# Perceiver block: reordering the first batch of an interval (statistics of x1, a state sum, norm rows and transposes)

## The chip, the cores and the metric

The kernel runs on one core of one Trainium2 chip. The metric is the device time of one execution in microseconds (us), as the median of several runs. Five engines with a queue each matter here: TensorE (PE, its weight loads are shown as PEld), VectorE (DVE), ScalarE (ACT), GpSimd (POOL) and SyncE (SP), which here only starts transfers. Each engine works through its own queue in order and waits on semaphores for the others.

## What is computed

```python
x = x + cross_attention(ctx, ctx, layernorm(x), mask)   # 64 batches, 32 rows, 257 keys, 16 heads of 32
x = x + mamba(layernorm(x))                             # below
x = x + quantised_ffn(layernorm(x))                     # 512 -> 2048 -> 512

# mamba: d_inner 1024, 16 states, over the 32 rows of each batch
x_, z = split(x @ in_proj_w)                            # 512 -> 2 * 1024
x_ = silu(causal_conv4(x_) + conv_b)
Bm, C, d = split(x_ @ x_proj_w)                         # 16, 16, 1
dt = softplus(d * dt_w + dt_b)
h[s] = exp(dt * A) * h[s-1] + (dt * x_) * Bm            # 16 states for each channel
y = sum_n(h * C) + x_ * D
out = (y * silu(z)) @ out_proj_w
```

## The kernel before

The 64 batches are 16 tiles of 4 batches (128 rows). Attention works batch by batch, mamba tile by tile. The two are interleaved by hand: `interval(ta, tm, to, more)` is one stretch in which the four batches `b = 0..3` of tile `ta` pass through attention, while tile `tm = ta - 1` begins mamba ("front") and tile `to = ta - 2` finishes it ("back"). The 16 intervals are followed by a hand-written tail and by the feed-forward part. Intervals 2 to 15 have both a front and a back. These are the 14 that the diff touches in full.

`schedule` is one function that every engine runs with its own class of parts (`Loads` for SP, `Products` for PE, `Functions` for ACT, `Side` for POOL, `Elementwise` for DVE). A part that an engine doesn't define does nothing there. So the order of the calls in `interval` is the order of the work in each of the five queues, and moving one call moves it in every queue that has a part of that name.

The scan of a tile goes by 8 chunks `c` of 128 channels. Each chunk has four steps on DVE, written (c, op): op 0 multiplies u with B (L1779), op 1 is the scan over 128x2048 elements (L1784), op 2 the product with C (L1790), op 3 the sum over the 16 states (L1756 twice and L1761). After op 2 POOL starts a transfer that adds one half of the states onto the other (L1527), so op 3 has 8 states left for all chunks but the last. `CHAIN` is the order of the 32 steps. `DONE` is a step's place in it, which the semaphore `scan_step` counts. Two chunk buffers alternate. `FINISH` and `BEGIN` say at which named place of which batch a step stands: `place("s")`, `place("a")` and so on. `FINISH_DECAYS` and `BEGIN_DECAYS` do the same for the exponentials of ACT (L1433) that feed op 1.

The parts that the diff moves, all in the first batch (`b == 0`):

- `mamba_norm(tm)`: DVE takes the statistics of x1 (BATCH_NORM_STATS L1577, BATCH_NORM_AGGREGATE L1582). POOL makes the inverse standard deviation and the shift out of them (`rstd`: L1488, L1490, L1493).
- `mamba_rows(tm)`: ACT writes the normed rows into `ln_out` (L1291).
- `mamba_turn`: PE transposes them into bank 5 (L1085). `mamba_transpose`: ACT copies them to `xn2T` (L1348). `mamba_in` (PE, L1092) multiplies them with the input weights; it waits for `xn2T` and for `keys_copy`.
- `keys_copy(g+1, 0)`: ACT copies half of the next batch's keys out of bank 6 (L1265).

Around them stand `x1_write` (DVE, L1693: attention's output plus residual), `load_bias` and `residual` (SP loads four bias rows, L789; POOL adds them to x, L1516, giving `xbo` for the next tile), `scores` (PE L1021, DVE score passes L1666), `softmax` (ACT exponentials L1286, then the DVE reciprocal L1679), `normalise` (ACT L1323), `kv_keys` (PE L988; POOL scales the mask, L1502), `kv_values` (PE L999), `transpose_p` (PE L1030) and `mamba_keep` (POOL copies x1 to x2, L1555).

Of the kernel before, what the change touches and what calls it, by code (L numbers as in the profile page):

```python
# [39 lines left out]
def perceiver_kernel(nc, x, ctx_kv, mask, Wq, bq, Wk, bk, Wv, bv, Wo, bo, Win, conv_w, conv_b, Wx,  # L40
# [13 lines left out]
    with ExitStack() as ctx:  # L54
# [270 lines left out]

        CHAIN = [(0, 0), (0, 1), (0, 2)]
        for c in range(1, IC):
            CHAIN += [(c, 0), (c, 1), (c, 2), (c - 1, 3)]
        CHAIN.append((IC - 1, 3))
        DONE = {step: k + 1 for k, step in enumerate(CHAIN)}  # L330
        FINISH = {(0, "a"): range(21, 22), (0, "b"): range(22, 26), (0, "c"): range(26, 28),
                  (1, "a"): range(28, 29), (1, "t"): range(29, 31), (1, "p"): range(31, 32)}
        BEGIN = {(1, "w"): range(0, 1), (1, "d"): range(1, 3), (1, "e"): range(3, 4), (2, "a"): range(4, 5),
                 (2, "b"): range(5, 7), (2, "c"): range(7, 9), (2, "d"): range(9, 11), (2, "e"): range(11, 12),
# [100 lines left out]
        def schedule(part, engine):  # L435
# [22 lines left out]
            def interval(ta, tm, to, more):  # L458

                here, front, back = ta is not None, tm is not None, to is not None  # L460
                for b in range(BT):
                    following = here and (b < BT - 1 or more)
                    g = ta * BT + b if here else None
                    keys = DC * (g + 2) if following else 0

                    def place(name):
                        if back:
                            part.decays(to, FINISH_DECAYS.get((b, name), ()))
                            part.scans(to, FINISH.get((b, name), ()))
                        if front:  # L470
                            part.decays(tm, BEGIN_DECAYS.get((b, name), ()))
                            part.scans(tm, BEGIN.get((b, name), ()))
                        if not front and not back:
                            part.weights_prepare(b, name)

                    if b == 0 and front:
                        part.x1_write(tm)
                    if b == 0 and here:
                        part.load_bias(ta)
                        part.residual(ta)  # L480
                    if following and 0 < b < BT - 1:
                        part.kv_turn(g + 1, 0, 0)
                    if here:
                        part.scores(g, ta, b, to)
                    if b == 0 and front:
                        part.mamba_norm(tm)
                    if b == 1 and front:
                        part.mamba_bcd(tm, keys - DC)
                    if following and 0 < b < BT - 1:
# [36 lines left out]
                        part.q_spread(ta + 1)  # L526
                    if following:
                        part.kv_keys(g + 1, b, ta, tm, to, more)
                    if following:
                        part.keys_copy(g + 1, 0)  # L530
                    if following and b == 0:
                        part.kv_values(g + 1, 0, range(0, 2))
                    if here:
                        part.normalise(g)
                    if b > 0:
                        place("n")
                    if b == 0 and front:
                        part.mamba_rows(tm)
                    if following:
                        part.keys_copy(g + 1, 1)  # L540
                    if b == 0 and front:
                        part.mamba_turn(tm, keys)
                        part.mamba_transpose(tm, keys)
                    if b == 0:
                        place("n")
                    place("k")
# [71 lines left out]
                    if b == 3 and here:  # L618
                        part.wo_product(ta, keys)

            interval(0, None, None, True)
            interval(1, 0, None, True)
            interval(2, 1, 0, True)
            with engine.Fori(3, NT - 1) as t:
                interval(t, t - 1, t - 2, True)
# [1377 lines left out]
```

## Time and profile before

| | |
|---|---|
| median of 3 runs | 2046.67 us (2040.75 to 2046.87) |
| the profiled execution | 2044.58 us, of which the span is 2042.8 us |
| mean granted TensorE clock | 0.977 |
| one interval in the steady part | about 110.2 us |

The profiled execution is 2.1 us below the median of the three and inside their range. Busy shares of the span: PE 93%, DVE 91%, ACT 82%, POOL 24%. A busy share doesn't say which engine sets the pace: for that the waits of each engine in one interval are read, and the timeline around the place that is changed. Below, "T" is the start of `x1_write` (L1693) in an interval.

### The profile page before, as it was taken

To read this page: it belongs to the slowest core of one execution; us is meant where nothing else is said; L and a number is where in the kernel's file an instruction comes from. 1 tells how busy PE (TensorE), PEld (TensorE's weight loads), DVE (VectorE), ACT (ScalarE), POOL (GpSimd) and SP (SyncE) were. 2 spreads that over 40 slices of the span, in tenths; PEclk is the share of its full clock that TensorE was granted. 3 is DMA by queue.
4 is the path that set the end of the run, shared out by engine and by line. 5 is a ranking of instruction groups with operands and counts; after the bars stand their busy time and mean duration, and the time that the engine had idled before them with its cause. 6 is when DMAs were issued, how large, how long until landed. Compare 5 with 4: busy or idle time off the path is not lost.

```text
span 2042.8 us, 37585 instructions
## 1 busy us (share of the span) xinstructions
PE 1907.6 (93%) x11658; PEld 1352.9 (66%) x11658; DVE 1850.1 (91%) x2315; ACT 1681.6 (82%) x4617; POOL 496.9 (24%) x397
## 2 busy tenths in 40 slices
PE   8898999999999999999999999999999999568799
PEld 5576776767676666767676767676667767366444
DVE  1546999999999999999999999999999999999778
ACT  3458989898988989898989898988989898876483
POOL 1001213041423223141314142423314141201013
PEclk9999999999999999999999999999999999788899
DMA  9523333333332333333333334233333233320214
GB/s 285 219 83 89 78 91 78 84 84 103 72 106 67 84 91 83 93 83 90 77 91 81 97 72 114 66 86 93 72 93 85 91 86 83 98 73 11 73 43 142
DMA packets 93395, 188.53 MB, mean 92 GB/s; under 512 B 18768, under 2 KB 39904, under 8 KB 88160
## 3 DMA queue, kind: packets, MB, share of 16 engines
q1 hardware_dynamic: 78448, 133.32, 20.2%
q0 software_dynamic: 14832, 54.01, 14.1%
q8 instruction: 32, 0.52, 0.1%
q14 instruction: 83, 0.68, 0.1%
HBM read 116.12 MB, written 17.18 MB: 65 GB/s over the span
## 4 chain that ended last, share of the span: by engine, by line
PE 43%; ACT 16%; DVE 12%; issue 11%; POOL 3%; SPq 1%; DMA 1%; DVEq 0%; POOLq 0%; ACTq 0%
PE bank L1092 10%; PE bank L999 8%; ACT dA L1433 7%; PE bank L1133 5%; PE bank L988 5%; DVE hb L1784 5%; PE bank L1196 3%; PE bank L1218 3%; PE bank L1039 2%; DVE hb L1779 2%; DVE hb L1756 2%; ACT xD L1417 2%; PE bank L1119 1%; POOL stats L1490 1%; DMA bo_sb<-bias_dram 1%
## 5 line engine op out<-in xcount | busy, mean ns | idle before, releaser
L1433 ACT ACTIVATE dA<-dt,A_sb 128x124 f32<-128x124 f32 x2048 | 617.1, 392 | 9.6 <-DVE dt L1734 8.4
L1784 DVE TENSOR_TENSOR_SCAN hb<-dA,hb 128x2048 f32<-128x2048 f32 x118 | 522.5, 4428 | 8.5 <-ACT dA L1433 4.8
L988 PE MATMUL bank<-ctxT,wk_sb 128*128 128x256 f32 x2048 | 463.1, 384 | 14.8 <-ACT ctxT L1249 11.4
L999 PE MATMUL bank<-wv_sb,ctxT 128*128 128x512 f32 x1024 | 465.4, 595 | 2.3 <-ACT ctxT L1249 2.3
L988 PEld LDWEIGHTS bank<-ctxT,wk_sb 128*128 128x128 f32 x2048 | 383.9, 191 | 78.9 <-ACT ctxT L1249 18.2
L999 PEld LDWEIGHTS bank<-wv_sb,ctxT 128*128 128x128 f32 x1024 | 186.7, 191 | 188.7 <-issue 185.3
L1527 POOL DMA_DIRECT2D hb<-hb x103 | 93.3, 906 | 861.5 <-DVE hb L1790 846.3
L1779 DVE TENSOR_TENSOR hb<-u,BC 128x2048 f32<-128x2048 f32 x118 | 270.4, 2291 | 5.7 <-DVE u L1746 2.6
L1790 DVE TENSOR_TENSOR hb<-hb,BC 128x2048 f32<-128x2048 f32 x117 | 268.9, 2298 | 1.5
L1092 PE MATMUL bank<-xn2T,win_sb 128*128 128x128 f32 x2048 | 237.9, 278 | 0.7 <-ACT xn2T L1348 0.7
L1092 PEld LDWEIGHTS bank<-xn2T,win_sb 128*128 128x128 f32 x2048 | 235.4, 194 | 4.2 <-issue 2.2
L1502 POOL TENSOR_SCALAR maskn<-maskb 128x257 f32<-128x257 f32 x64 | 140.2, 2191 | 270.1 <-DVE soft L1666 267.7
L1756 DVE TENSOR_TENSOR hb<-hb 128x512 f32<-128x512 f32 (+2 forms) x248 | 149.7, 604 | 4.6
L1039 PEld LDWEIGHTS bank<-PT,V 128*128 128x128 f32 x1024 | 124.8, 194 | 35.2 <-issue 35.2
L1272 ACT COPY V<-bank 128x512 f32<-128x512 f32 x128 | 75.0, 586 | 77.0 <-PE bank L1039 55.7
L1286 ACT ACTIVATE Pr<-Pr,soft 128x257 f32<-128x257 f32 x256 | 127.3, 510 | 12.1 <-DVE soft L1666 11.9
L1249 ACT ACTIVATE ctxT<-bank,lastT 128x256 f32<-128x256 f32 x256 | 102.3, 474 | 36.5 <-PE bank L954 34.3
L1265 ACT ACTIVATE KT<-bank,bqkv 128x256 f32<-128x256 f32 x256 | 106.2, 467 | 29.7 <-PE bank L988 28.5
L1039 PE MATMUL bank<-PT,V 128*128 128x128 f32 x1024 | 127.5, 278 | 2.0 <-ACT PT L1340 2.0
L1323 ACT ACTIVATE Pr<-Pr,soft 128x256 f32<-128x256 f32 x256 | 109.2, 506 | 14.0 <-DVE soft L1679 14.0
L1720 DVE SCALAR_TENSOR_TENSOR xs<-xpad,convw,xs 128x128 f32<-128x128 f32 x384 | 103.7, 347 | 14.7 <-ACT xs L1367 14.2
L1666 DVE CUSTOM_DVE_ANT_0 Pr<-bank,maskn 128x257 f32<-128x257 f32 x256 | 93.2, 421 | 17.7 <-PE bank L1021 17.5
(159 smaller groups left out, 2581.5 us busy)
## 6 DMA issues: line engine op xcount, KB each, us to landing
hb<-hb POOLq DMA_DIRECT2D x103, 512.0 KB, 4.8
ctx_sb<-in_ctx_dram SPq DMA_DIRECT2D x64, 512.0 KB, 3.7
BC<-bcd_dram SPq DMA_DIRECT2D x32, 1024.0 KB, 7.2
maskb<-in_mask_Bx1x1xS_fk_dram SPq DMA_DIRECT2D x64, 128.5 KB, 3.4
wstage<-in_L_ffn_w_dram SPq DMA_DIRECT2D x4, 2048.0 KB, 11.2
x_sb<-in_x_dram SPq DMA_DIRECT2D x16, 256.0 KB, 3.4
win_sb<-in_L_attn_in_proj_w_dram SPq DMA_DIRECT2D x1, 4096.0 KB, 24.3
bo_sb<-bias_dram SPq DMA_DIRECT2D x64, 64.0 KB, 2.0
```

The lines of the kernel that those rows point to most:

```text
L988: last = pe.matmul(bank[6 + j][:, (m % 2) * KF:(m % 2 + 1) * KF], wk_sb[:, c, m * P:(m + 1) * P], ctxT[:, c, :], start=(c == 0), stop=(c = ...
L999: last = pe.matmul(bank[h][:], ctxT[:, c, h * P:(h + 1) * P], wv_sb[:, c, :], start=(c == 0), stop=(c == DC - 1))
L1039: last = pe.matmul(bank[4][:, m * P:(m + 1) * P], V[:, h, m * P:(m + 1) * P], PT[:, h, m, :], start=(h == 0), stop=(h == 1))
L1092: last = pe.matmul(bank[6 + q % 2][:, e * P:(e + 1) * P], win_sb[:, c, n:n + P], xn2T[:, c, :], start=(c == 0), stop=(c == DC - 1))
L1286: act.activation(Pr[:, m, :], Pr[:, m, :], ACT.Exp, scale=-1.0, bias=soft[:, 0, m:m + 1], accum_out=soft[:, 1, m:m + 1]).then_inc(exp_done, 1)
L1323: act.mul(Pr[:, m, 0:KF], Pr[:, m, 0:KF], soft[:, 2, m:m + 1]).then_inc(p_ready, 1)
L1433: last = act.activation(dA[:, c % 2, n * BT:(n + 1) * BT, 1:], dt[:, c, :].rearrange("p (b s) -> p b s", s=S)[:, :, 1:], ACT.Exp, scale=A_ ...
L1502: pool.tensor_scalar(maskn[:], maskb[:], -NEG, 1.0, ALU.mult, ALU.mult).then_inc(mask_scaled, 1)
L1756: dve.tensor_tensor(tile[:, 0:n, :], tile[:, 0:n, :], tile[:, n:2 * n, :], ALU.add).then_inc(sum_step, 1)
L1779: ins = dve.tensor_tensor(tile, u[:, c, :].unsqueeze(1).broadcast_to([P, NS, P]), BC[:, 0:NS, :], ALU.mult)
L1784: ins = dve.tensor_tensor_scan(flat, dA[:, c % 2].rearrange("p n s -> p (n s)"), flat, 0.0, ALU.mult, ALU.add)
L1790: ins = dve.tensor_tensor(tile, tile, BC[:, NS:2 * NS, :], ALU.mult)
```

## The change

In the first batch of an interval the statistics of x1 (`mamba_norm`) come right behind `x1_write`, ahead of `residual` and of the score passes. The sum of chunk 4 stands ahead of the product with C of chunk 5, at the place "s" between the score passes and the reciprocal. The normed rows (`mamba_rows`) come right behind the exponentials on ACT, ahead of `normalise`; their transposes on PE come ahead of the first half of `kv_values`, and the copy to `xn2T` ahead of `keys_copy(g+1, 1)`. For that `keys_copy(g+1, 0)` moves behind `normalise` in the first batch; in the other batches its order against the engines' other work is as before.

```diff
         for c in range(1, IC):
-            CHAIN += [(c, 0), (c, 1), (c, 2), (c - 1, 3)]
+            CHAIN += [(c, 0), (c, 1), (c - 1, 3), (c, 2)] if c == 5 else [(c, 0), (c, 1), (c, 2), (c - 1, 3)]
...
-        FINISH = {(0, "a"): range(21, 22), (0, "b"): range(22, 26), (0, "c"): range(26, 28),
+        FINISH = {(0, "s"): range(21, 22), (0, "a"): range(22, 23), (0, "b"): range(23, 26), (0, "c"): range(26, 28),
...
                     if b == 0 and front:
                         part.x1_write(tm)
+                        part.mamba_norm(tm)
...
                     if here:
                         part.scores(g, ta, b, to)
-                    if b == 0 and front:
-                        part.mamba_norm(tm)
...
                     if following:
                         part.kv_keys(g + 1, b, ta, tm, to, more)
-                    if following:
-                        part.keys_copy(g + 1, 0)
+                    if b == 0 and front:
+                        part.mamba_rows(tm)
+                        part.mamba_turn(tm, keys)
                     if following and b == 0:
                         part.kv_values(g + 1, 0, range(0, 2))
+                    if b > 0 and following:
+                        part.keys_copy(g + 1, 0)
                     if here:
                         part.normalise(g)
+                    if b == 0 and following:
+                        part.keys_copy(g + 1, 0)
                     if b > 0:
                         place("n")
                     if b == 0 and front:
-                        part.mamba_rows(tm)
+                        part.mamba_transpose(tm, keys)
                     if following:
                         part.keys_copy(g + 1, 1)
-                    if b == 0 and front:
-                        part.mamba_turn(tm, keys)
-                        part.mamba_transpose(tm, keys)
```

## Rows read from the trace of the kernel before

**Rows 1.** Busy time by interval: stretch, length, then each engine; one steady interval.

```profile
562.00:672.00 110.00, 106.48 (x663) 76.30 (x662) 107.15 (x134) 98.44 (x281) 31.08 (x24) 1.00 0.34 86
```

**Rows 2.** Waits of DVE, 562 to 672 us: total, times, longest.

```profile
DVE soft L1679 <- ACT Pr L1286: 0.7, 1, 0.7
...
DVE u L1746 <- DVE zs L1863: 0.2, 1, 0.2
```

**Rows 3.** Chain that ended last, 560 to 675 us: start, length, what.

```profile
574.69 0.66 POOL xbo L1516
```

**Rows 4.** Timeline of DVE from 572 us: start, length, engine, line.

```profile
572.31 0.67 DVE L1693 TENSOR_TENSOR x<-bank,xbo 128x512 f32<-128x512 f32 x1
...
572.89 0.42 DVE L1666 CUSTOM_DVE_ANT_0 Pr<-bank,maskn 128x257 f32<-128x257 f32 x1
...
574.27 0.69 DVE L1577 BATCH_NORM_STATS2 stats<-x 128x6 f32<-128x512 f32 x1
...
575.11 0.18 DVE L1582 BATCH_NORM_AGGREGATE stats<-stats 128x2 f32<-128x6 f32 x1
...
575.97 0.18 DVE L1679 RECIPROCAL soft<-soft 128x4 f32<-128x4 f32 x1 [0.68 <-ACT Pr L1286]
576.09 2.29 DVE L1790 TENSOR_TENSOR hb<-hb,BC 128x2048 f32<-128x2048 f32 x1
...
578.30 1.15 DVE L1756 TENSOR_TENSOR hb<-hb 128x512 f32<-128x512 f32 x2
...
579.80 2.29 DVE L1779 TENSOR_TENSOR hb<-u,BC 128x2048 f32<-128x2048 f32 x1
```

**Rows 5.** The same timeline: ACT and PE around the transposes.

```profile
573.86 0.51 ACT L1286 ACTIVATE Pr<-Pr,soft 128x257 f32<-128x257 f32 x1
...
576.54 1.71 ACT L1323 ACTIVATE Pr<-Pr,soft 128x256 f32<-128x256 f32 x4
...
577.64 1.88 PE L999 MATMUL bank<-wv_sb,ctxT 128*128 128x512 f32 x4
...
580.67 0.63 PE L1085 MATMUL bank<-idf,ln_out 128*128 128x128 f32 x4 [1.15 <-ACT ln_out L1291]
...
581.42 0.59 ACT L1348 COPY xn2T<-bank 128x512 f32<-128x512 f32 x1 [0.27 <-PE bank L1085]
...
582.15 7.38 PE L1092 MATMUL bank<-xn2T,win_sb 128*128 128x128 f32 x64
```

**Rows 6.** Timeline, 1289 to 1296 us: from a tile's statistics to POOL's power.

```profile
1291.42 0.18 DVE L1582 BATCH_NORM_AGGREGATE stats<-stats 128x2 f32<-128x6 f32 x1 [0.15 <-DVE stats L1577]
...
1291.79 2.46 POOL L1490 TENSOR_TENSOR stats<-stats,consts 128x1 f32<-128x1 f32 x1
```

**Rows 7.** Timeline, 653 to 673 us: score pass, its exponential, and rstd on POOL.

```profile
654.79 0.42 DVE L1666 CUSTOM_DVE_ANT_0 Pr<-bank,maskn 128x257 f32<-128x257 f32 x1
655.04 0.57 POOL L1490 TENSOR_TENSOR stats<-stats,consts 128x1 f32<-128x1 f32 x1
...
655.25 0.51 ACT L1286 ACTIVATE Pr<-Pr,soft 128x257 f32<-128x257 f32 x1 [0.39 <-DVE soft L1666]
...
655.82 0.26 POOL L1493 TENSOR_SCALAR stats<-stats 128x1 f32<-128x1 f32 x1 [0.21 <-POOL stats L1490]
```

**Rows 8.** Timelines where POOL and DVE meet: 241, 353, 564 and 2006 us.

```profile
241.29 1.27 POOL L1516 TENSOR_TENSOR xbo<-x_sb,bo_sb 128x512 f32<-128x512 f32 x1 [7.70 <-DVE x L1693]
...
353.21 2.96 DVE L1790 TENSOR_TENSOR hb<-hb,BC 128x2048 f32<-128x2048 f32 x1
...
564.52 0.93 POOL L1555 COPY x<-x 128x512 f32<-128x512 f32 x1
...
2006.42 1.05 DVE L1952 TENSOR_TENSOR w1qT<-w1qT 128x512 f32<-128x512 f32 x1
```

**Rows 9.** Durations of two DVE lines: count, ns min/median/max, first and last start.

```profile
L1761 DVE TENSOR_TENSOR u<-hb x117: 291/293/1128, 197.7 to 1786.3; 128x128 f32<-128x128 f32 x117
...
L1952 DVE TENSOR_TENSOR w1qT<-w1qT x16: 691/693/1477, 1989.4 to 2039.6; 128x512 f32<-128x512 f32 x16
```

## The prediction

> **What bounds the kernel now.** I read the busy time by interval first, then the waits inside one interval, then the chain, and last the timeline around T (the start of `x1_write`). In a steady interval PE is busy 106.5 of 110 us and DVE 107.2 [rows 1]. The two are too close for the shares to decide, so the waits must. DVE waits 0.7 us for ACT's exponentials before the reciprocal, and otherwise only for itself (0.2 us, the next largest) [rows 2]. PE waits 1.15 us for `ln_out` at the transposes alone [rows 5]. So DVE has about 0.7 us in each interval that another engine could give back, and PE has more. The chain runs through the place of the change: POOL makes `xbo` once the bias rows have landed, and only then come rstd, the normed rows and the transposes [rows 3]. That chain is one of several that are nearly tied. Since DVE hardly ever idles, its own queue is what an edit must shorten. I take DVE as the pace of intervals 2 to 15.
>
> **DVE before.** From T (572.31) to the multiply of chunk 6 (579.80) are 7.49 us [rows 4]: `x1_write`, four score passes, statistics, 0.68 us of waiting, reciprocal, product (5,2), sum (4,3).
>
> **DVE after, if nothing interferes.** `x1_write` takes 0.67; the statistics must now wait for it, and such a handover between dependent instructions costs some 0.04 (my estimate; bounds 0 and the 0.15 between the two statistics instructions [rows 6]). Then 0.69 + 0.15 + 0.18, so the statistics end at T+1.73. Four score passes take 1.38 (572.89 to 574.27), to T+3.11. The sum takes 1.50 from its start to the next start (578.30 to 579.80), some 0.1 less when the next instruction doesn't need it: T+4.5. Reciprocal 0.12, product 2.21 (576.09 to 578.30) [rows 4]: the multiply of chunk 6 starts at T+6.84, which is 0.65 earlier. The score passes were queued far ahead before and now stand behind a wait; I bound this by 0 and 0.15. The gain is 0.5 to 0.65.
>
> **Does the sum cover the wait?** A score pass starts 0.46 before its exponential when ACT is free [rows 7], so the exponentials start at T+2.2. From the first one to the reciprocal are 2.11 us (573.86 to 575.97) [rows 4, 5], so the reciprocal could go at T+4.3, with DVE busy until T+4.5. The wait of 0.68 is covered. The later score passes cost ACT only 0.6 us, since it was busy with decays until 573.86 anyway.
>
> **POOL.** rstd no longer stands behind `residual`. Statistics end to power takes 0.19 (1291.60 to 1291.79) [rows 6], the power 0.57, a gap 0.21, the last step 0.26 [rows 7]: rstd ends at T+2.96, where before PE stood waiting for the rows made from it until T+8.36 (580.67) [rows 5]. But `residual`, which ran from T+2.4 beside score passes and statistics, is now queued behind it. Its bias rows have landed by then (it ran from 574.69) [rows 3], so its 128x512 addition, 1.27 us long, runs from T+3.0 to T+4.25. Nobody waits for `xbo` soon. What matters is what DVE does then: the sum of chunk 4 starts at T+3.1.
>
> **What a large POOL operation costs DVE.** Beside score passes `xbo` costs nothing: 1.27 us at 241.29, and the passes keep their 0.42 [rows 4, 8]. Beside a DVE operation that reads two tensors from SBUF it costs much. The last add of a sum takes 0.29 us, but 1.13 where POOL's copy of 0.93 us starts within 0.03 us of it [rows 8, 9]; 14 of 117 are stretched so. It ends as if it had started 0.1 to 0.15 us before the end of the copy. And in one interval `xbo` itself came late, at 352.75: the product took 2.96 instead of 2.29 [rows 4, 8]. By the same reading the sum's first add now effectively starts at T+4.10 instead of T+3.1 to 3.25. It costs 0.85 to 1.0.
>
> The Trainium skill ("SBUF — State Buffer", Who interferes with whom) says that a DVE instruction with two SBUF inputs contends with a GpSimd instruction that reads SBUF, that whichever starts first keeps the port for the whole instruction, and that a DVE instruction with at most one SBUF input doesn't contend. The rows of `xbo` beside score passes, whose other input is in PSUM, agree. Where page and rows differ is the price: by the page DVE would wait for the whole 1.27 us, and the sum below would be 0.15 us an interval larger, +7.0 us in all.
>
> **Sum.** T+4.10 + 1.4 (sum) + 0.12 + 2.21 = T+7.83 against T+7.49: DVE loses 0.35 us an interval. Over 14 intervals this is +4.9 us. Their waits before the reciprocal are not all 0.7, and one of them already had the stretched product; I take these as cancelling within a microsecond. Interval 1 and the tail are taken at zero: interval 1 has no back, DVE idles there for many microseconds, and the tail isn't edited.
>
> **PE and ACT.** The normed rows follow the exponentials at about T+4.4 and end at T+5.2. `kv_keys` ends at T+5.33 (577.64), so the transposes follow it with hardly a wait, and the 1.15 us of idle PE time go [rows 5]. `normalise` waits for the reciprocal at T+5.6 and runs 1.7 us; then come `keys_copy` (two operations of the same width as `normalise`'s four, so 0.85) and the copy to `xn2T` (0.6) [rows 5]: `mamba_in` starts at about T+8.9 instead of T+9.84 (582.15). So PE is 0.9 us earlier, and what lies behind it (xpad, taps, convolution) is not late. Neither ACT nor PE becomes the bound; what they gain turns into waits for DVE, since DVE's queue sets the pace. `keys_copy(g+1, 0)` is some 2 us later, and it is next needed by `mamba_in` and by the scores of b = 1, 17 us on. I cost it at nothing.
>
> **Other queues.** SP's order is unchanged. POOL's transfer for chunk 5 is issued behind its product, some 0.4 us later, and the sum that needs it is 15 us away. The sum of chunk 4 comes 2.9 us earlier than before, but its transfer was issued at T-8. The scaled mask follows the transfer and still meets the multiply of chunk 6, as before.
>
> **Rivals.**
> 1. *The gain arrives.* POOL and DVE pass each other (`xbo` is held until the reciprocal or lands between instructions), and DVE keeps 0.5 to 0.65 us: -7 to -9 us. For it: the port is taken by whoever is first, and all depends on 0.1 us. Against it: I find no free 1.27 us on DVE before the product.
> 2. *The sum wins the port.* It starts before `xbo`, which is held and then takes a slice at the boundary between two adds. Such held operations stretch the next one by 0.36 (1.05 instead of 0.69) [rows 8, 9]. DVE then gains 0.15 to 0.3: -2 to -4 us.
> 3. *Slower.* The same mechanism at its worst. It gets dearer the closer behind the start of `xbo` the sum wants to start: if rstd ends 0.1 to 0.25 us later than I reckon while `xbo` is still first, the add is held until T+4.4. That is 0.3 more an interval, +0.65 x 14 = +9 us. It decides from a start of `xbo` at about T+3.1.
> 4. *PE was the pace* (through `ln_out`, as the chain suggests), and the whole 0.9 to 1.1 us come back: -13 to -15 us. Against it stands that DVE waits for others only 0.7 us in an interval.
> 5. *The change doesn't do what it says*: rstd early, but the normed rows don't come earlier, since ACT holds them back. They follow the exponentials directly, so I give this nothing of its own.
>
> **Numbers.** The profiled execution had 2044.58 us: 2044.6 + 4.9 = 2049.5. The median of three is 2.1 above it, which would give 2051.6. I say 2050. Chances: the forecast 0.42 (its own range 2047 to 2053), the gain 0.17, the sum first 0.17, slower 0.18, PE as the pace 0.06. The range is to leave out PE as the pace and the far ends of rivals 1 and 3: 2038 to 2056. A measurement of this kernel can tell about 0.3%, 6 us, from no change. Slower by more than that are rival 3 and a quarter of the forecast, 0.29; faster rival 4 and most of rival 1, 0.19; within it the rest, 0.52.
>
> **What the profile after would show.** DVE's wait before the reciprocal in batch 0 gone (right if below 0.1). The first add of the sum in batch 0 at 1.5 to 1.7 us instead of 0.69, beside `xbo` that starts at T+3.0. PE's wait for `ln_out` below 0.3. `mamba_in` at T+8.9. An interval of 110.5 us. It is wrong if the add keeps its 0.69 (rival 1: interval 109.6), if `xbo` itself is stretched beyond 1.27 (rival 2: 110.0), or if DVE idles elsewhere for ACT or PE, so that its queue wasn't the pace.

## The result and the profile after

| | before | after |
|---|---|---|
| median of 9 runs each | 2044.73 us (2040.75 to 2046.87) | 2049.48 us (2048.53 to 2053.39) |
| the profiled execution, its span | 2044.58 us, 2042.8 us | 2053.39 us, 2051.6 us |

The changed kernel takes 1.0028 times the time of the kernel before, with a 95% interval of 1.0018 to 1.0037: 4.75 us slower by the medians. The profiled execution of the changed kernel is the slowest of its nine, so the two profiles stand further apart (8.8 us in the spans) than the medians.

The busy time in one steady interval of the changed kernel (columns as in [rows 1]):

```profile
1238.12:1348.94 110.82, 106.81 (x664) 76.40 (x663) 108.30 (x134) 98.43 (x282) 27.99 (x24) 1.00 0.35 86
```

The interval is 110.8 us instead of 110.1 to 110.2. DVE's work has grown by 1.1 us (107.2 in [rows 1]), though its instructions are the same 134. The waits of one interval from T, DVE first and PE behind it (total, times, longest; they answer to [rows 2]):

```profile
DVE Pr L1667 <- issue: 0.4, 1, 0.4
DVE stats L1583 <- DVE stats L1578: 0.3, 2, 0.2
...
PE bank L989 <- ACT Q L1317: 0.8, 1, 0.8
PE bank L1120 <- ACT xs L1375: 0.4, 1, 0.4
PE bank L1093 <- ACT xn2T L1349: 0.4, 1, 0.4
```

DVE's wait for the exponentials is gone, as forecast. In its place stand 0.4 us before the first score pass, with "issue" as the cause: nothing that the profile shows held it. PE no longer waits a microsecond for `ln_out`, and has small new waits elsewhere, for ACT. The timeline of DVE from T = 1348.94 (it answers to [rows 4]; the columns are start, length, engine, line):

```profile
1348.94 0.67 DVE L1694 TENSOR_TENSOR x<-bank,xbo 128x512 f32<-128x512 f32 x1
1349.64 0.69 DVE L1578 BATCH_NORM_STATS2 stats<-x 128x6 f32<-128x512 f32 x1
1350.49 0.18 DVE L1583 BATCH_NORM_AGGREGATE stats<-stats 128x2 f32<-128x6 f32 x1 [0.15 <-DVE stats L1578]
...
1351.05 0.43 DVE L1667 CUSTOM_DVE_ANT_0 Pr<-bank,maskn 128x257 f32<-128x257 f32 x1 [0.38 <-issue]
...
1352.44 1.75 DVE L1757 TENSOR_TENSOR hb<-hb 128x512 f32<-128x512 f32 x1
...
1354.68 0.29 DVE L1762 TENSOR_TENSOR u<-hb 128x128 f32<-128x128 f32 x1
...
1354.89 0.17 DVE L1680 RECIPROCAL soft<-soft 128x4 f32<-128x4 f32 x1
...
1354.98 2.26 DVE L1791 TENSOR_TENSOR hb<-hb,BC 128x2048 f32<-128x2048 f32 x1
...
1357.16 2.28 DVE L1780 TENSOR_TENSOR hb<-u,BC 128x2048 f32<-128x2048 f32 x1
```

And POOL, ACT and PE in the same stretch:

```profile
1350.95 0.23 POOL L1489 TENSOR_SCALAR stats<-stats 128x1 f32<-128x1 f32 x1 [8.87 <-DVE stats L1583]
...
1351.27 0.57 POOL L1491 TENSOR_TENSOR stats<-stats,consts 128x1 f32<-128x1 f32 x1
...
1352.05 0.27 POOL L1494 TENSOR_SCALAR stats<-stats 128x1 f32<-128x1 f32 x1 [0.21 <-POOL stats L1491]
...
1352.37 1.27 POOL L1517 TENSOR_TENSOR xbo<-x_sb,bo_sb 128x512 f32<-128x512 f32 x1
...
1353.50 0.80 ACT L1292 ACTIVATE ln_out<-x,stats 128x512 f32<-128x512 f32 x1
1354.55 0.63 PE L1086 MATMUL bank<-idf,ln_out 128*128 128x128 f32 x4
...
1358.14 7.38 PE L1093 MATMUL bank<-xn2T,win_sb 128*128 128x128 f32 x64 [0.37 <-ACT xn2T L1349]
```

The reader is to see one pair: POOL's addition for `xbo` starts at T+3.43 and keeps its 1.27 us. The first add of the moved sum starts 0.07 us behind it and takes 1.75 us instead of 0.69 ([rows 9] have the same shape at 0.69). The multiply of chunk 6 starts at T+8.22, where it was at T+7.49 [rows 4] and in the second half of the trace before at T+7.48. The rows come at T+4.56, the transposes at T+5.61 instead of T+8.36, `mamba_in` at T+9.20 instead of T+9.84 [rows 5]. PE has what it was to get, and the kernel is slower.

### The profile page after: what moved, and what is told of

Read it like the earlier page. It is cut to its first block, busy times and chain, and to the rows that moved or that the text cites. A ratio compares the mean times of both kernels' runs of the same rounds, so it can differ in the third digit from the quotient of the medians.

```text
span 2051.6 us, 37558 instructions
## 1 busy us (share of the span) xinstructions
PE 1911.0 (93%) x11643; PEld 1353.3 (66%) x11658; DVE 1863.1 (91%) x2315; ACT 1679.7 (82%) x4617; POOL 451.8 (22%) x397
## 4 chain that ended last, share of the span: by engine, by line
PE 31%; DVE 29%; issue 23%; ACT 2%; DVEq 1%; DMA 0%; POOL 0%; POOLq 0%; ACTq 0%
DVE hb L1785 9%; DVE hb L1780 6%; PE bank L1093 5%; PE bank L989 5%; PE bank L1134 5%; PE bank L1000 5%; DVE hb L1757 5%; DVE xs L1721 3%; PE bank L1197 3%; PE bank L1219 3%; DVE u L1762 2%; DVE Pr L1667 1%; PE bank L1120 1%; PE bank L1040 1%; PE bank L1167 1%
## 5 line engine op out<-in xcount | busy, mean ns | idle before, releaser
L1434 ACT ACTIVATE dA<-dt,A_sb 128x124 f32<-128x124 f32 x2048 | 616.8, 391 | 12.7 <-DVE dt L1735 11.5
L1503 POOL TENSOR_SCALAR maskn<-maskb 128x257 f32<-128x257 f32 x64 | 125.3, 1958 | 269.5 <-DVE soft L1667 267.1
L1757 DVE TENSOR_TENSOR hb<-hb 128x512 f32<-128x512 f32 (+2 forms) x248 | 164.4, 663 | 4.9 <-DMA hb<-hb 0.3
L1721 DVE SCALAR_TENSOR_TENSOR xs<-xpad,convw,xs 128x128 f32<-128x128 f32 x384 | 103.1, 346 | 13.7 <-ACT xs L1368 13.4
L1489 POOL TENSOR_SCALAR stats<-stats 128x1 f32<-128x1 f32 x48 | 52.1, 1086 | 282.9 <-DVE stats L1583 282.9
## 6 DMA issues: line engine op xcount, KB each, us to landing
wstage<-in_L_ffn_w_dram SPq DMA_DIRECT2D x4, 2048.0 KB, 11.4
```

The costliest lines, as they stand in the source:

```text
L1434: last = act.activation(dA[:, c % 2, n * BT:(n + 1) * BT, 1:], dt[:, c, :].rearrange("p (b s) -> p b s", s=S)[:, :, 1:], ACT.Exp, scale=A_ ...
L1503: pool.tensor_scalar(maskn[:], maskb[:], -NEG, 1.0, ALU.mult, ALU.mult).then_inc(mask_scaled, 1)
L1721: dve.scalar_tensor_tensor(acc, src, tap, acc, ALU.mult, ALU.add).then_inc(conv_done, 1)
L1757: dve.tensor_tensor(tile[:, 0:n, :], tile[:, 0:n, :], tile[:, n:2 * n, :], ALU.add).then_inc(sum_step, 1)
```

## The experiments

All times are medians, each with its ratio to the kernel before on the same chip. T is the start of `x1_write` in an interval. The theory: DVE's queue is the pace, and the addition on POOL takes from it what the edit gave. The rivals: the new order of PE and ACT costs the time, the residual addition matters by its place in the chain before the rows, or PE is the pace.

**e4: the changed kernel with a one-column `xbo`.** The residual of the other columns is left out, from tile 1 on.

```diff
-                        pool.tensor_tensor(xbo[:], x_sb[:], bo_sb[:], ALU.add).then_inc(xbo_ready, 1)
+                        pool.tensor_tensor(xbo[:, 0:1], x_sb[:, 0:1], bo_sb[:, 0:1], ALU.add).then_inc(xbo_ready, 1)
```

> The changed kernel, but POOL adds bias and x for the first column only (the residual of the other 511 columns is left out, from tile 1 on). Order, waits and transfers are the same; only the length of the one POOL operation beside the sum goes, from 1.27 us to about 0.2. By the collision: 1.0 us less an interval, 13 to 15 us below the changed kernel, 8 to 11 below the kernel before in the profile. By the order of PE and ACT or by the statistics standing ahead: no more than 2 us below the changed kernel.

Measured: 2035.29 us, 0.9957 of before (0.9943 to 0.9971). That is 14 us below the changed kernel. POOL and DVE in its timeline:

```profile
1230.98 0.19 POOL L1517 TENSOR_TENSOR xbo<-x_sb,bo_sb 128x1 f32<-128x1 f32 x1
...
1231.05 1.15 DVE L1757 TENSOR_TENSOR hb<-hb 128x512 f32<-128x512 f32 x2
```

Both adds of the sum together take 1.15 us, where the changed kernel's take 2.21. The start is the same 0.07 us behind `xbo`. With the length of one POOL operation gone, everything else left as changed, the loss turns into a gain. The order of PE and ACT and the early statistics are still in this kernel, so neither can be what made the changed kernel slower than the kernel before.

**e1: the addition moved to where DVE leaves the port free.** The bias rows are loaded in the last batch of the interval before, and the addition goes ahead of rstd.

```diff
                     if b == 0 and front:
                         part.x1_write(tm)
-                        part.mamba_norm(tm)
                     if b == 0 and here:
-                        part.load_bias(ta)
+                        if isinstance(ta, int) and ta < 2:
+                            part.load_bias(ta)
                         part.residual(ta)
+                    if b == 0 and front:
+                        part.mamba_norm(tm)
...
+                    if b == 3 and here and more and not (isinstance(ta, int) and ta == 0):
+                        part.load_bias(ta + 1)
                     if b == 3 and back:
                         part.out_transpose(to, keys)
```

> The changed kernel, but with the residual addition back ahead of rstd on POOL, and with its four bias rows loaded at the end of the interval before (for the tiles from 2 on), so that the addition can start right behind x1_write, at T+0.8, and is over at T+2.1, before the sum of chunk 4 wants to start at T+3.5. PE's and ACT's order stay as changed. If the collision on the port of POOL and DVE makes the changed kernel slow: the first add of the sum is back from 1.76 to 0.69 us, DVE saves 1.07 us in each of 14 intervals, 13 to 15 us less than the changed kernel, some 5 to 10 below the kernel before. If the new order of PE and ACT (keys copied later, PE waiting for xn2T) is what costs: as slow as the changed kernel. If PE was the pace: 13 to 15 us below the kernel before.

Measured: 2036.06 us, 0.996 (0.9945 to 0.9974), 13.4 below the changed kernel and 8 below the kernel before. From T = 1335.38:

```profile
1336.38 1.27 POOL L1521 TENSOR_TENSOR xbo<-x_sb,bo_sb 128x512 f32<-128x512 f32 x1 [7.86 <-DVE x L1698]
...
1338.87 1.15 DVE L1761 TENSOR_TENSOR hb<-hb 128x512 f32<-128x512 f32 x2
...
1342.53 2.29 DVE L1784 TENSOR_TENSOR hb<-u,BC 128x2048 f32<-128x2048 f32 x1
```

The addition runs T+1.00 to T+2.27 beside the statistics and a score pass, and these keep their 0.69 and 0.42 us. The sum follows at T+3.49 unhindered. The interval is 109.75 us. All the work is done here, and the gain is e4's.

**e3: the sum back behind the product.** CHAIN and FINISH as before the change, all else as changed.

> The changed kernel with the sum of chunk 4 back behind the product (CHAIN and FINISH as before). Now the residual addition on POOL, T+3.4 to T+4.7, meets a DVE that waits for the exponentials. If DVE's queue is the pace: the add keeps its 0.69, but DVE waits 1.2 us before the reciprocal, the multiply of chunk 6 starts at T+8.5 instead of T+8.2, and the time is 3 to 6 us above the changed kernel. If PE is the pace: no slower than the changed kernel, since the transposes come as early as there.

Measured: 2055.25 us, 1.0051 (1.0037 to 1.0065), 5.8 above the changed kernel. Its DVE waits and its multiply of chunk 6 (T = 1239.55):

```profile
DVE soft L1680 <- ACT Pr L1287: 1.1, 1, 1.1
...
1248.07 2.29 DVE L1780 TENSOR_TENSOR hb<-u,BC 128x2048 f32<-128x2048 f32 x1
```

With nothing to do between the score passes and the reciprocal, DVE idles 1.1 us, and the multiply starts at T+8.52. PE's transposes come at T+5.6 as in the changed kernel, and it doesn't help. Moving the sum is worth 0.3 us an interval even with the collision. The early statistics without the sum, with the rest as changed, cost DVE 1.0 us: T+8.52 against T+7.48.

**e2: the sum alone.** CHAIN and FINISH as changed, all else as before.

> The kernel before with the sum of chunk 4 moved ahead of the product alone (CHAIN and FINISH). The score passes come at once behind x1_write, the statistics behind them, so the sum starts at T+3.0. The residual addition starts at T+2.0 to T+2.4 as before and overlaps the first 0.3 to 0.65 us of it. If DVE's queue is the pace: the wait of 0.68 for the exponentials goes, 0.15 to 0.5 of it is given back by the stretched add, so 0.2 to 0.5 less an interval, 3 to 7 us below the kernel before. If PE is the pace by way of the normed rows: no change, since PE and POOL wait as before.

Measured: 2099.68 us, 1.027 (1.0256 to 1.0285). This missed by 60 us, and neither theory had it. The first guess was the addition, which still overlaps the sum here. The next kernel takes it away.

**e5: the sum alone, with the bias rows early.** The diffs of e2 and, for the bias rows, of e1.

> The kernel before with the sum of chunk 4 ahead of the product, as in e2, and with the bias rows loaded an interval early, so that the residual addition on POOL is over at T+2.1, before the sum starts. The statistics stay behind the score passes, PE and ACT are as before. If the sum alone lost its time because the last one-column step of rstd on POOL, ready at about T+4.7, is held off the port by the product and the multiply that now follow each other without a gap: no help from the early bias rows; the step still ends at T+9 or later, and the time is 2085 to 2105 us. If it was lost to the residual addition beside the sum: some 2036 to 2040.

Measured: 2086.54 us, 1.0204 (1.0189 to 1.0219). With the addition out of the way 13 of e2's 55.5 us come back, where no help was expected; the other 42 stay. POOL and DVE in its timeline (T = 1258.56), and one interval's waits of DVE and PE:

```profile
1263.39 4.20 POOL L1496 TENSOR_SCALAR stats<-stats 128x1 f32<-128x1 f32 x1 [0.21 <-POOL stats L1493]
...
1263.08 2.26 DVE L1793 TENSOR_TENSOR hb<-hb,BC 128x2048 f32<-128x2048 f32 x1
1265.26 2.28 DVE L1782 TENSOR_TENSOR hb<-u,BC 128x2048 f32<-128x2048 f32 x1
...
DVE xs L1723 <- ACT xs L1370: 3.0, 2, 2.2
...
PE bank L1088 <- ACT ln_out L1294: 2.9, 1, 2.9
```

The last step of rstd works on one element in each partition and takes 0.26 us [rows 7]. Here it takes 4.20. It starts 0.31 us behind the product and ends with the multiply. In the second half of the kernel before it took 2.4 us:

```profile
1237.42 2.29 DVE L1790 TENSOR_TENSOR hb<-hb,BC 128x2048 f32<-128x2048 f32 x1
...
1238.00 2.36 POOL L1493 TENSOR_SCALAR stats<-stats 128x1 f32<-128x1 f32 x1 [0.21 <-POOL stats L1490]
...
1239.63 1.14 DVE L1756 TENSOR_TENSOR hb<-hb 128x512 f32<-128x512 f32 x2
```

The sum followed the product there, and the step ended at 1240.36, where one add waits for the other. In e2 and e5 the multiply follows, which depends on nothing just before it, and starts without a gap. In e5 the rows come at T+9.07, PE waits 2.9 us, `mamba_in` starts at T+11.6 to T+12.7, and then the convolution on DVE waits 1.8 to 4.5 us for ACT's taps. So DVE is the pace only as long as the rows are in time.

**e9: e5 with one wait more.**

```diff
                             dve.wait_ge(scan_step, 4 * IC * t + DONE[c, 1])
...
+                            if c == 5:
+                                dve.wait_ge(ln_rstd[1], 3 * (t + 2))
                             ins = dve.tensor_tensor(tile, tile, BC[:, NS:2 * NS, :], ALU.mult)
```

> e5 with one wait more: DVE doesn't start the product of chunk 5 before rstd on POOL has ended. If the product and the multiply behind it hold the last step of rstd off the port: the step takes 0.3 us instead of 4.2, the product starts 0.6 to 0.8 us later than in e5, the multiply of chunk 6 at T+7.4 instead of T+6.7, the transposes 3 us earlier, DVE's waits for the taps go, and the time falls by more than 40 us to 2038 to 2046, though DVE waits more. If rstd was late for another reason: as slow as e5 or slower, 2086 to 2095.

Measured: 2038.32 us, 0.997 (0.9958 to 0.9981): 48 us faster than e5, by a wait added to the busiest queue. POOL's step and the product:

```profile
1233.89 0.26 POOL L1496 TENSOR_SCALAR stats<-stats 128x1 f32<-128x1 f32 x1 [0.21 <-POOL stats L1493]
...
1234.19 2.29 DVE L1795 TENSOR_TENSOR hb<-hb,BC 128x2048 f32<-128x2048 f32 x1 [0.52 <-POOL stats L1496]
```

DVE gives 0.52 us and gets back more than 3. That settles what e5 lost, and what e2 lost beyond e5 was the addition. It also shows what the early statistics in the changed kernel are good for: they end rstd at T+3.4, before the product, so that the sum can be moved without such a wait.

**e6: the bias rows early and nothing else.** The kernel before with that part of e1's diff.

> The kernel before, with nothing changed but that the bias rows are loaded an interval early and the residual addition runs at T+0.8 instead of T+2.0 to T+2.4. This takes away the first link of the chain that ended last (bias rows, addition, rstd, rows, transposes). If DVE's queue is the pace: no change beyond 0.15%, also where the rows come earlier. If that chain is the pace: rstd starts 0.5 us earlier in an interval, 5 to 7 us less, or more where its last step gets in ahead of the product and the rows come 2 us earlier.

Measured: 2039.38 us, 0.9978 (0.9969 to 0.9987). This missed too: I had expected less than 0.15%, and it is 0.22% faster. The starts of `x1_write` in the traces say where. In the steady part the kernel before has 110.11 to 110.13 us and e6 110.10. But the kernel before has one interval of 112.15 us (from 349.93), the one with the product stretched to 2.96 [rows 8] and a wait of 1.1 us for the taps, and then five of 110.17 to 110.24. It also has one of 110.79 (from 1122.86), where the wait before the reciprocal is 1.33 us. e6 has none of these: its longest is 110.13. So the steady pace didn't change with the chain's first link gone, as the theory says. What went is a late arrival of the bias rows, which had put the addition beside the product once. In the 110.79 interval they were late too (`xbo` at T+2.86), but that this lengthened it, or the five slightly longer ones, is not shown.

**e7: e1 with the rows and transposes in the old order.** PE's and ACT's part of the change undone.

> e1 with the normed rows, their transposes, the copy to xn2T and the copies of the keys in the order of the kernel before. Statistics ahead, sum ahead and early bias rows stay. If DVE's queue is the pace: as fast as e1 within 0.15%, since mamba_in starts near T+9.5, as in the kernel before, where DVE never waited for it. If the earlier transposes are worth something: slower than e1 by 5 us or more.

Measured: 2036.72 us, 0.9962 (0.9948 to 0.9976): as fast as e1. The transposes come at T+7.93 instead of T+5.6, and DVE's multiply in both at T+7.15. In a steady interval, then, norm rows and transposes ahead are worth at most 0.04 us. One of e7's 14 intervals, though (from 1118.43), took 111.53 us instead of 109.79. DVE's largest wait in it:

```profile
DVE xs L1723 <- ACT xs L1370: 0.9, 1, 0.9
```

PE ended `kv_keys` 2.6 us later than in its neighbours, at T+8.15, the transposes came at T+9.70, and DVE waited for the taps. e1 has no such interval. Why PE was late there is open, and so is whether the new order would have absorbed it.

**e8: e1 with the statistics woven into the score passes.** On DVE: pass, BATCH_NORM_STATS, pass, BATCH_NORM_AGGREGATE, two passes. The heart of the diff on top of e1 (`norm_first` and `norm_second` are the two statistics instructions with their waits):

```diff
                     for m in range(DC):
                         self.score_pass(g, m)
+                        if norm is not None and m == 0:
+                            self.norm_first(norm)
+                        if norm is not None and m == 1:
+                            self.norm_second(norm)
```

> e1 with the two statistics instructions woven in between the score passes (pass, BATCH_NORM_STATS, pass, BATCH_NORM_AGGREGATE, two passes), so that no dependent pair stands next to another. If the 0.04, 0.15 and 0.38 us of idle DVE time around the statistics lie on the path: the sum starts at T+2.9 instead of T+3.5, 0.55 to 0.65 less an interval, 7 to 9 us below e1, near 2028 us. If something else than DVE is the bound by then (ACT's exponentials, the rows, the taps): less than 3 us below e1, or slower if a step of rstd is held behind the product.

Measured: 2024.64 us, 0.9907 (0.9892 to 0.9921): 11.4 below e1, 19 below the kernel before on its chip. The gain is larger than the 7 to 9 us expected. From T = 1327.95:

```profile
1328.53 0.41 DVE L1675 CUSTOM_DVE_ANT_0 Pr<-bank,maskn 128x257 f32<-128x257 f32 x1
...
1328.87 0.69 DVE L1725 BATCH_NORM_STATS2 stats<-x 128x6 f32<-128x512 f32 x1
...
1329.81 0.18 DVE L1731 BATCH_NORM_AGGREGATE stats<-stats 128x2 f32<-128x6 f32 x1
...
1330.66 1.15 DVE L1782 TENSOR_TENSOR hb<-hb 128x512 f32<-128x512 f32 x2
...
1334.32 2.29 DVE L1805 TENSOR_TENSOR hb<-u,BC 128x2048 f32<-128x2048 f32 x1
```

The sum starts at T+2.71 instead of T+3.49: besides the gaps of 0.03, 0.15 and 0.38 us, instructions that don't depend on each other overlap by some 0.1 where one follows another (the first pass starts at T+0.58, though `x1_write` takes 0.66). This is the fastest kernel of the study, with all the work done.

**All of them in one table.** Where DVE doesn't wait for the taps, the interval follows from one point of DVE's queue. The first eight rows are a steady interval; the last two leave out the first and last of the 14:

| kernel | multiply of chunk 6 at | interval | difference | median, us |
|---|---|---|---|---|
| e8 | T+6.37 | 108.97 | 102.60 | 2024.64 |
| e1 | T+7.15 | 109.75 | 102.60 | 2036.06 |
| e4 | T+7.15 | 109.76 | 102.61 | 2035.29 |
| e7 | T+7.15 | 109.79 | 102.64 | 2036.72 |
| e9 | T+7.33 | 109.92 | 102.59 | 2038.32 |
| before, second half | T+7.48 | 110.11 | 102.63 | 2044.73 |
| changed | T+8.22 | 110.83 | 102.61 | 2049.48 |
| e3 | T+8.52 | 111.14 | 102.62 | 2055.25 |
| e5 | T+6.7 to T+6.9 | 112.0 to 114.7 | | 2086.54 |
| e2 | T+7.0 to T+7.6 | 112.6 to 115.1 | | 2099.68 |

The rest of the interval is 102.59 to 102.64 us in eight kernels, while `mamba_in` moves between T+8.4 and T+9.4. That is DVE's queue as the pace. The last two rows are its limit.

## Why the prediction was right, step by step

**The pace: right.** The table above shows it. PE got its transposes 2.2 to 2.75 us earlier and the kernel slowed down. Rival 4 has fallen, and e7's steady intervals say the same from the other side.

**The wait before the reciprocal: right.** It is gone, and e3 shows it at 1.1 us without the sum there.

**The collision: right, and the whole of the loss.** In 12 of the 14 intervals the first add takes 1.75 to 1.78 us, beside an `xbo` of 1.27. The forecast was 1.5 to 1.7. The kernels without the collision, e4 and e1, are 14.2 and 13.4 us faster than the changed kernel, about 14 times the 1.06 us (14.8).

**Terms that were mis-sized.** Two were, and both lie in how long a queue takes to start its next instruction behind a wait. The score passes behind the statistics start 0.38 us late in 12 of the 14 intervals; I had bounded this by 0.15. And POOL begins the power 0.60 us after the statistics (1350.67 to 1351.27), not 0.19. The 0.19 came from a place where POOL was still busy with the instruction before; from idle it takes longer. Both shifted the pair by 0.4 us and left it together: the sum starts at T+3.50 instead of T+3.1 to 3.25, `xbo` at T+3.43 instead of T+3.0. So the add effectively starts at T+4.56 (its end less 0.69) instead of T+4.10. The loss is 0.73 us in a steady interval, not 0.35. The forecast interval was 110.5 us; 110.83 was measured. In a steady interval that is the price of rival 3 (0.65), by its own mechanism: dearest where the sum wants to start just behind `xbo`.

**Why the total is still near the forecast: by luck.** 4.75 us measured between the medians, 4.9 forecast, but not by the same terms. The cause and the direction were foreseen; that the sizes meet is chance. From the first to the last of the 15 `x1_write` the traces have 1543.1 us before and 1549.1 after: 6.0 in 14 intervals, 0.43 each. The kernel before has 2.1 us in one interval that the changed one doesn't have (the stretched product and a wait for the taps; with `xbo` queued behind rstd in every interval, its start no longer depends on the bias rows), is 0.7 slower than its neighbours in another, and 0.1 in five more. I had taken such differences as cancelling. The two errors go against each other, and the 1.2 us between 6.0 and 4.75 are less than the executions of one kernel differ by (6.1 and 4.9 us in the table of the result). The other 2.8 us between the spans lie before the first and behind the last of these starts. Up to the first one e3 has the code of the changed kernel and reaches it 1.3 us earlier, so at least that much is variation from run to run.

**Rival 2 had the wrong price.** In the first and last of the 14 intervals the score passes started 0.15 us behind the statistics and not 0.38, as I had bounded it, and there the sum came first, by 0.02 us:

```profile
1684.69 2.10 DVE L1757 TENSOR_TENSOR hb<-hb 128x512 f32<-128x512 f32 x2
...
1684.71 1.79 POOL L1517 TENSOR_TENSOR xbo<-x_sb,bo_sb 128x512 f32<-128x512 f32 x1
```

`xbo` is held 0.5 us and then takes the boundary between the two adds: 2.10 us for both instead of 1.15. Being first saved DVE 0.1 us, not 0.6. The price of 0.36 that I took from [rows 8] belongs to an operation that had 0.5 us left when DVE's add wanted to start (2004.85 + 2.08 against 2006.42).

**PE and ACT.** The transposes follow `kv_keys` with almost no wait, as forecast. `mamba_in` starts at T+9.2 instead of T+8.9, since the reciprocal is later by the same 0.4. As forecast, nothing behind it was late.

**The other queues: right about this change, blind for its parts.** POOL's steps of rstd are ahead of the product here. Had the statistics stayed where they were, the sum's move would have cost 42 to 56 us (e5, e2). The prediction didn't see that the sum's move needs rstd to be over before the product, by the early statistics or by a wait as in e9.

## What to carry to other kernels

Before a long operation is put into an idle gap of a saturated VectorE, look at what GpSimd does in that gap. Its small steps may have lived on it, and a full tile operation beside a two-input VectorE operation can cost VectorE nearly its own length (here 1.06 us for 1.27). Place GpSimd's tile operations beside VectorE work that reads at most one tensor from SBUF (here the statistics and the score passes, which kept their length), by loading their operands early if need be. Put independent instructions between dependent ones: the woven order gave 11 us on top of everything else.

## What the runs showed of the hardware beyond the expected

- A one-column GpSimd step that becomes ready 0.3 us behind the start of a VectorE product is held through that product and through the next, independent operation: 4.20 us instead of 0.26. With dependent adds behind, as in the kernel before, it gets in after the first: 2.36 us.
- A VectorE instruction behind a wait for the statistics, with several semaphore instructions ahead of it in the queue, starts 0.38 us after the engine is free in a steady interval, and 0.15 in the first and last; what makes the difference is not shown. GpSimd takes 0.28 us from the end of the statistics to its first step and 0.60 to its second.
- The VectorE add that starts 0.07 us behind a GpSimd addition of 1.27 us ends as if it had started 0.14 us before the end of that addition (1353.50 against 1353.64). That lies within the 0.1 to 0.15 read from [rows 9].
